# A transformer megakernel on one core: windowed attention's transposed scores as three float32r passes, with GpSimd making the low parts

## The chip, the cores and the metric

The kernel runs on one NeuronCore of a Trainium2 chip. The metric is the device time of one execution in microseconds; less is better. The time before is 2594.16 us, the median of three runs (2591.99 to 2595.44).

## The reference, cut to what matters

Six residual blocks run one after the other over 16 sequences of 256 tokens with 128 features. The change touches the first and the third, which are the same two-layer stack with windowed attention (8 heads of 64, window 64). Per layer:

```python
qkv = shift_token(x) @ wqkv
q, k = l2norm(q) * qs, l2norm(k) * ksc
q, k = rotary_xpos(q, k)                      # cosines, sines, a scale by position
sim = einsum('bhwid,bhwjd->bhwij', bq, bk)    # window of 64 queries, its 64 keys and the 64 before
sim = where(mask, -finfo.max, sim)
out = einsum('bhwij,bhwjd->bhwid', softmax(sim), bv)
x = x + out @ wo
h = layernorm(shift_token(x)) @ w1 + b1       # then a * gelu(g) @ w2 + b2, added to x
```

The other blocks (an attention with a distance bias, two mixtures of experts and a linear attention) are left as they are, but for one tile's place in memory.

## The kernel before, in words

Everything is laid out by hand: each engine has its own program, and semaphores order them. The feed-forward stage `ffn(f)` runs twice (f = 0 and 1). It walks over 32 items each time: layer 0 of the 16 sequences, then layer 1 of them. An item passes through three steps of the loop at once: in step k the engines project queries, keys and values of item k (`new`), do the attention of item k-1 (`mid`) and the feed-forward part of item k-2 (`old`). In layer 0, `pre` also normalises the input of a coming sequence. The order inside a step is written out in the loops at the end of each engine's `ffn`.

One step, as far as the change and the steps of the prediction touch it:

- TensorE turns (transposes) the rotated keys and queries of item i-1 (`qk_T`, L1284 and L1292) into PSUM, projects the first half of item i (`qk`, L1273 to L1275, float32r in three passes), projects the attention's output of item i-2 (`proj`, L1407), and computes plain scores (`scores`, L1329 masks, L1334 products in bf16), from which only the row maxima are taken.
- VectorE copies turned keys out of PSUM to `kT` (float32, L870) and from there to bf16, `kb` (L871), and raises `f_kb`. ScalarE copies turned queries to `qT` (L585) and to bf16, `qb` (L586), and raises `f_qsb`. Then ScalarE copies the projections of item i (`copy_qk`, L565).
- VectorE then does in this order: cosines of half 0 (L884), the residual (`resid`, L933), maxima of the plain scores (`s_max`, L908 and L913) with `y_center` (L939) between, the split of the maxima into two bf16 parts (`m_split`, L921 and L922), `y_normed` (L943), sums of squares (L890), `m_out` (L927), cosines of half 1 (L884), sums, `clip` (L895), `gated` (L950), two `qk_norm` (L901) and others.
- GpSimd multiplies by the sines (`sines`, L466, two instructions per half) and adds to the cosines (`rotated`, L474) for both halves of item i, and then splits the next item's input into a high and a low part (`split_h`, L491 and L493), ahead of which in layer 0 stands `normed` (L481).
- TensorE goes on with the feed-forward `up` (L1425), which waits for `y_normed`, and with the transposed scores (`scores_T`). For three groups of heads and columns it first adds offsets and masks in bf16 (`offsets`, L1355 and L1357), then the products `kT` by `qT` (`products`, L1363). These are float32 matmuls on 64 rows; two neighbouring heads lie on the two halves of the array. Offsets of group 2 wait for `gated`. Then come `down` (L1436) and the sums over the values (`attend`, L1388 and L1396), for which ScalarE makes exponentials (L593) of the transposed scores.

`link` is a helper that makes an engine wait for its own last instruction; `free(engine, semaphore, n)` is a wait that is left out for n <= 0. L1741 and L1739 belong to the linear attention, L818 to the preparation of weights.

Of the kernel before, what the change touches and what calls it, by code (L numbers as in the profile page):

```python
# [17 lines left out]
F32 = mybir.dt.float32  # L18
I32 = mybir.dt.int32
F32R = mybir.dt.float32r  # L20
BF16 = mybir.dt.bfloat16
# [7 lines left out]
P = 128  # L29
# [95 lines left out]
def build(nc, io, at):  # L125
    ctx = ExitStack()
    with ctx:
        def sb(name, shape, dt=F32, on=ctx):
            return on.enter_context(nc.sbuf_tensor(name, shape, dt))

        def sem(name):
            return ctx.enter_context(nc.semaphore(name))
# [64 lines left out]
        N_STAGE = at["slope_eye"][1]  # L197
        hh = [sb(f"h_hi{n}", [P, T], F32R) for n in range(2)]
        hl = [sb(f"h_lo{n}", [P, T], F32R) for n in range(2)]
        with ExitStack() as early:  # L200
            stage = sb("stage", [P, N_STAGE], on=early)
        scl = sqs[:, 0:8 * DH].rearrange("p (l g c d) -> p l g c d", l=DEPTH, g=2, c=2)
        with ExitStack() as ffn_small:
            kb, qb = sb("kT_bf", [P, 4, T], BF16, ffn_small), sb("qT_bf", [P, 4, T], BF16, ffn_small)
            V = [sb(f"v{n}", [P, TILES, INNER], F32, ffn_small) for n in range(2)]
            OT = sb("o_T", [P, 4, T], F32, ffn_small)
            G = sb("gelu", [P, HC, T], F32, ffn_small)
            U = sb("gated", [P, HC, T], F32, ffn_small)
        q_slots = [sb(f"q_slots{n}", [P, 4, T], F32R) for n in range(3)]
# [9 lines left out]
        with ExitStack() as ffn_only:  # L219
# [36 lines left out]
        wbuf = [work[0][:, EW * n:EW * (n + 1)] for n in range(5)]  # L256
        xtile = [sb(f"tile_x{n}", [P, HW]) for n in range(6)]
        xT = [sb(f"tile_xT{n}", [P, P]) for n in range(2)]
        gT = [sb(f"tile_g{n}", [P, EC, P]) for n in range(3)]
        yrow = [sb(f"tile_y{n}", [P, D]) for n in range(4)]  # L260
        o1, o2, o3 = 0, 4 * P, 4 * P + 2 * HC * P

# [17 lines left out]
        lbw, fold, chain = sem("lbw"), sem("fold"), sem("chain")  # L280
        f_y0, f_h, f_qk, f_cp, f_sq, f_cos, f_sin, f_sum, f_ss, f_ssm, f_rn, f_nrm = [sem(f"ffn_{n}") for n in
            ("y0", "h_split", "qk", "qk_sb", "sq", "cos", "sin", "rot", "ss", "ss_max", "rnorm", "qk_norm")]
        f_vsb, f_kT, f_qT, f_kb, f_qsb, f_s, f_smax, f_mlo, f_mT, f_mTs = [sem(f"ffn_{n}") for n in
            ("v_sb", "kT", "qT", "k_bf", "qT_sb", "s", "s_max", "m_lo", "mT", "mT_sb")]
        f_st, f_p, f_den, f_o, f_rec, f_on, f_proj, f_res = [sem(f"ffn_{n}") for n in
            ("st", "p", "den", "o", "rec", "o_norm", "proj", "resid")]
        f_mean, f_cen, f_lsq, f_var, f_rstd, f_norm, f_up, f_g, f_u, f_down, f_res2 = [sem(f"ffn_{n}") for n in
# [152 lines left out]
        def _(pool):  # L440
# [17 lines left out]
            def ffn(f):  # L458
                def sines(i, t):
                    l, _ = layer_of(i)  # L460
                    a = rA[:, t, :].rearrange("p (g h d) -> p g h d", g=2, h=HEADS)
                    b = rB[:, t, :].rearrange("p (g h d) -> p g h d", g=2, h=HEADS)
                    pool.wait_ge(f_cp, 2 * i + t + 1)
                    for h in range(2):
                        o_, i_ = slice(32 * h, 32 * h + 32), slice(32 - 32 * h, 64 - 32 * h)
                        last = pool.tensor_tensor(b[:, :, :, o_], a[:, :, :, i_],  # L466
                                                  tab[:, l, 1, t, :, o_].unsqueeze(2).to_broadcast([P, 2, HEADS, 32]),
                                                  ALU.mult)
                    last.then_inc(f_sin, 1)

                def rotated(i, t):
                    pool.wait_ge(f_sin, 2 * i + t + 1)
                    pool.wait_ge(f_cos, 2 * i + t + 1)
                    pool.tensor_tensor(rC[:, t, :], rC[:, t, :], rB[:, t, :], ALU.add).then_inc(f_sum, 1)  # L474

                def normed(s):
                    n = f * SEQS + s
                    free(pool, f_sum, 2 * (f * ITEMS + s))
                    pool.wait_ge(o_rstd, n + 1)
                    for h, (r, c) in enumerate(halves()):  # L480
                        pool.tensor_tensor(Y[r, s, c], ocen[r, :], osq[r, :], ALU.mult).then_inc(f_y0, 1)  # L481
                        pool.wait_ge(f_y0, 2 * n + h + 1)

                def split_h(i):
                    l, s = layer_of(i)
                    if l == 0:
                        pool.wait_ge(f_y0, 2 * (f * SEQS + s + 1))
                    else:
                        pool.wait_ge(f_res2, i - SEQS + 1)
                    free(pool, f_qk, 3 * (i - 1))  # L490
                    pool.tensor_copy(hh[i % 2][:, :], Y[:, s, 0:T]).then_inc(f_h, 1)  # L491
                    pool.wait_ge(f_h, 2 * i + 1)
                    pool.tensor_tensor(hl[i % 2][:, :], Y[:, s, 0:T], hh[i % 2][:, :].bitcast(F32), ALU.subtract)\  # L493
                        .then_inc(f_h, 1)

                for k in range(-1, ITEMS):
                    i = f * ITEMS + k
                    for t in range(TILES):
                        if k >= 0:
                            sines(i, t)  # L500
                            rotated(i, t)
                    if k + 1 < SEQS:
                        normed(k + 1)
                    if k + 1 < ITEMS:
                        split_h(i + 1)
# [44 lines left out]
        def _(act):  # L550
# [8 lines left out]
            def ffn(f):  # L559
# [21 lines left out]

                def copy_q(i):
                    act.wait_ge(f_qT, i + 1)
                    q = PS[:, 3:5, :]
                    act.activation(qT.rearrange("p (b c) t -> p b (c t)", b=2), q, ACT.Copy)  # L585
                    act.activation(qb[:, :, :].rearrange("p (b c) t -> p b (c t)", b=2), q, ACT.Copy).then_inc(f_qsb, 1)  # L586

                def exps(i, n):
                    act.wait_ge(f_st, 3 * i + n + 1)
# [217 lines left out]
        def _(dve):  # L807
# [59 lines left out]
            def ffn(f):  # L867
                def k_out(i):
                    dve.wait_ge(f_kT, i + 1)
                    link(dve.tensor_copy(kT.rearrange("p (b c) t -> p b (c t)", b=2), PS[:, 5:7, :]))  # L870
                    dve.tensor_copy(kb[:, :, :], kT).then_inc(f_kb, 1)  # L871

                def o_norm(i, a):
                    dve.wait_ge(f_o, 2 * i + a + 1)
# [379 lines left out]
        def _(pe):  # L1254
# [22 lines left out]
            def ffn(f):  # L1277
# [42 lines left out]
                def scores(i):  # L1320
# [10 lines left out]
                    for bs, hs, w, t, k0, _ in groups:  # L1331
                        for h in hs:
                            r, o = slice(64 * (h % 2), 64 * (h % 2) + 64), (h - hs[0]) // 2 * w
                            last = pe.matmul(PS[:, bs[h % 2], o:o + w], qb[r, h // 2, t * P:(t + 1) * P],  # L1334
                                             kb[r, h // 2, k0:k0 + w], start=False, stop=True, skip_group_check=True)
                        last.then_inc(f_s, 1)

                def m_T(i):
# [8 lines left out]
                def scores_T(i):  # L1347
# [10 lines left out]
                                      start=False, stop=False, skip_group_check=True)  # L1358

                    def products(bs, hs, w, j, i0, m):  # L1360
                        for h in hs:
                            r, o = slice(64 * (h % 2), 64 * (h % 2) + 64), (h - hs[0]) // 2 * w
                            last = pe.matmul(PS[:, bs[h % 2], o:o + w], kT[r, h // 2, j * P:(j + 1) * P],  # L1363
                                             qT[r, h // 2, i0:i0 + w], start=False, stop=True, skip_group_check=True)
                        last.then_inc(f_st, 1)

                    pe.wait_ge(f_mTs, i + 1)
                    pe.wait_ge(f_cp, min(2 * i + 4, 2 * ITEMS * (f + 1)))
                    offsets(*groups[0])
                    pe.wait_ge(f_vsb, min(i + 2, ITEMS * (f + 1)))  # L1370
# [449 lines left out]
```

## Time and profile before

| | |
|---|---|
| median of three runs | 2594.16 us |
| profiled execution, its own time | 2591.7 us |
| its span | 2589.9 us |
| TensorE busy | 2277.1 us, 88% |
| VectorE busy | 1718.9 us, 66% |
| ScalarE busy | 1463.9 us, 57% |
| GpSimd busy | 1089.9 us, 42% |

The span runs from the first to the last instruction of the profiled execution. The shares of busy time are averages over stages of different kinds; the two feed-forward stages lie at about 80 to 900 us and 1310 to 2125 us. In the views PE is TensorE, PEld its weight loads, DVE VectorE, ACT ScalarE, POOL GpSimd. A float32 matmul stands in the trace as two rows of instructions, a float32r or bf16 matmul as one.

### The profile page before, as it was taken

How to read it: one execution, taken by the hardware profiler on the slowest of the kernel's cores; microseconds unless marked ns; L12 is line 12 of the kernel's file. 1: busy time of each engine (PE TensorE's matmuls, PEld its weight loads, DVE VectorE, ACT ScalarE, POOL GpSimd, SP SyncE). 2: the span in 40 equal slices, each digit the busy share in tenths (PEclk: the TensorE clock that was granted, in tenths of full speed). 3: DMA queues.
4: the chain of work that ended last, by engine and by line, in shares of the span. 5: the costliest groups of instructions: out<-in, count | busy, mean ns of one | idle time of the engine just before them, and what ended most of it. 6: DMA issues, size and time to landing. Idle time of an engine off the chain costs nothing. (4 is left out here: it accounts for less than half of the span.)

```text
span 2589.9 us, 52641 instructions
## 1 busy us (share of the span) xinstructions
PE 2277.1 (88%) x21574; PEld 1715.4 (66%) x21574; DVE 1718.9 (66%) x2800; ACT 1463.9 (57%) x2382; POOL 1089.9 (42%) x800
## 2 busy tenths in 40 slices
PE   2799999999999779999789999999999984878576
PEld 1577777777777556666457777777777753766266
DVE  3677777777777457777367777777877844533544
ACT  0567676666666425556456767666666642434332
POOL 4655555565565100000065555556556504410432
PEclk8899999999999889999989999999999987999899
DMA  7000000089999000000000000000000012110013
GB/s 147 1 1 1 2 2 1 1 91 115 108 122 109 8 1 2 2 2 2 1 1 2 1 1 2 2 2 1 2 2 2 1 54 60 56 53 1 29 51 99
DMA packets 185425, 73.63 MB, mean 28 GB/s; under 512 B 79658, under 2 KB 181204, under 8 KB 185060
## 3 DMA queue, kind: packets, MB, share of 16 engines
q1 hardware_dynamic: 177172, 56.68, 18.3%
q0 software_dynamic: 5568, 10.12, 1.3%
q10 hardware_dynamic: 2448, 3.48, 0.6%
q8 instruction: 173, 2.83, 0.5%
q14 instruction: 64, 0.52, 0.1%
HBM read 24.05 MB, written 46.18 MB: 27 GB/s over the span
## 5 line engine op out<-in xcount | busy, mean ns | idle before, releaser
L466 POOL TENSOR_TENSOR work<-work,rot_tables 128x512 f32<-128x512 f32 x256 | 446.9, 1767 | 451.3 <-ACT work L565 451.3
L474 POOL TENSOR_TENSOR work<-work 128x1024 f32<-128x1024 f32 x128 | 305.2, 2385 | 13.0 <-DVE work L884 3.1
L884 DVE TENSOR_TENSOR work<-work,rot_tables 128x1024 f32<-128x1024 f32 x128 | 163.9, 1281 | 112.1 <-ACT work L565 112.1
L1039 DVE TENSOR_REDUCE small<-psum 128x4 f32<-128x1024 f32 x128 | 156.6, 1223 | 91.1 <-PE psum L1545 91.0
L1273 PE MATMUL psum<-qkv_w_hi,h_hi 128*128 128x512 f32 x384 | 182.8, 476 | 18.8 <-POOL h_lo L493 16.3
L1425 PE MATMUL psum<-centered,ffn_w 128*128 128x256 f32 x768 | 191.1, 400 | 6.5 <-DVE centered L943 2.9
L901 DVE TENSOR_TENSOR work<-work,small 128x1024 f32<-128x1024 f32 x128 | 159.6, 1249 | 51.2 <-ACT small L579 47.0
L676 ACT ACTIVATE work<-psum 128x1024 f32<-128x1024 f32 x128 | 131.1, 1024 | 100.5 <-PE psum L1552 100.5
L481 POOL TENSOR_TENSOR y_all<-centered,squared 64x256 f32<-64x256 f32 x64 | 48.3, 755 | 308.2 <-ACT squared L625 305.6
L1363 PE MATMUL psum<-work 64*128 64x128 f32 (+1 forms) x2048 | 175.8, 311 | 0.0
L1425 PEld LDWEIGHTS psum<-centered,ffn_w 128*128 128x128 f32 x768 | 146.2, 197 | 37.4 <-DVE centered L943 18.7
L1363 PEld LDWEIGHTS psum<-work 64*128 64x128 f32 x2048 | 144.7, 188 | 32.6 <-issue 32.6
L731 ACT ACTIVATE tile_g<-psum,work 128x128 f32<-128x128 f32 x312 | 89.0, 368 | 136.3 <-PE psum L1674 105.0
L1396 PE MATMUL psum<-work,v 128*32 128x192 f32 (+1 forms) x4096 | 162.6, 299 | 0.0
L593 ACT ACTIVATE work<-psum 128x768 f32<-128x768 f32 (+1 forms) x192 | 154.9, 872 | 5.4 <-PE psum L1363 5.1
L535 POOL DMA_INDIRECT h_area<-rows,position x64 | 62.5, 977 | 221.1 <-DVE position L1125 200.8
L890 DVE TENSOR_REDUCE small<-qk_squares 128x16 f32<-128x1024 f32 x128 | 154.7, 1209 | 0.4 <-ACT qk_squares L570 0.4
L1274 PE MATMUL psum<-qkv_w_lo,h_hi 128*128 128x512 f32 x384 | 153.4, 399 | 0.0
L1275 PE MATMUL psum<-qkv_w_hi,h_lo 128*128 128x512 f32 x384 | 153.1, 399 | 0.0
L585 ACT ACTIVATE work<-psum 128x1024 f32<-128x1024 f32 x64 | 65.7, 1026 | 144.6 <-PE psum L1292 144.6
L565 ACT ACTIVATE work<-psum 128x1024 f32<-128x1024 f32 x128 | 130.3, 1018 | 22.3 <-PE psum L1275 21.5
L570 ACT ACTIVATE qk_squares<-work 128x1024 f32<-128x1024 f32 x128 | 135.3, 1057 | 2.0
(280 smaller groups left out, 5695.2 us busy)
## 6 DMA issues: line engine op xcount, KB each, us to landing
h_area<-mean_weights SPq DMA_DIRECT2D x16, 2048.0 KB, 27.2
tile_x<-h_area SPq DMA_DIRECT2D x78, 64.5 KB
work<-y_tokens SPq DMA_DIRECT2D x8, 512.0 KB, 6.1
stage<-in_consts ACTq DMA_DIRECT2D x1, 3009.0 KB, 12.7
work<-in_x SPq DMA_DIRECT2D x4, 512.0 KB, 28.3
expert_w<-in_ew SPq DMA_DIRECT2D x1, 2048.0 KB
expert_w<-in_ew SPq DMA_DIRECT2D x8, 256.0 KB
out<-work SPq DMA_DIRECT2D x8, 256.0 KB, 3.5
```

The lines of the kernel that those rows point to most:

```text
L466: last = pool.tensor_tensor(b[:, :, :, o_], a[:, :, :, i_], tab[:, l, 1, t, :, o_].unsqueeze(2).to_broadcast([P, 2, HEADS, 32]), ALU.mult)
L474: pool.tensor_tensor(rC[:, t, :], rC[:, t, :], rB[:, t, :], ALU.add).then_inc(f_sum, 1)
L593: act.activation(PT[:, hs, a:a + w].rearrange("p (h b) j -> p b h j", b=2), PS[:, bs, 0:m * w].rearrange("p b (h j) -> p b h j", h=m), ACT ...
L884: dve.tensor_tensor(g(rC[:, t, :]), g(rA[:, t, :]), tab[:, l, 0, t, :, :].unsqueeze(2).to_broadcast([P, 2, HEADS, DH]), ALU.mult)\
L890: dve.tensor_reduce(sm[0][:, 16 * t:16 * t + 16], sq[:, t, :].rearrange("p (g d) -> p g d", d=DH), AX, ALU.add).then_inc(f_ss, 1)
L901: dve.tensor_tensor(c_, c_, sm[0][:, 96 + 16 * t:112 + 16 * t].unsqueeze(2).to_broadcast([P, 16, DH]), ALU.mult).then_inc(f_nrm, 1)
L1039: dve.tensor_reduce(dst, PS[:, 0:2, :].rearrange("p b (t j) -> p b t j", t=TILES), AX, ALU.max, negate=True).then_inc(a_smax, 1)
L1273: pe.matmul(out, hi, w_hi, start=True, stop=False)
L1274: pe.matmul(out, hi, w_lo, start=False, stop=False)
L1363: last = pe.matmul(PS[:, bs[h % 2], o:o + w], kT[r, h // 2, j * P:(j + 1) * P], qT[r, h // 2, i0:i0 + w], start=False, stop=True, skip_gro ...
L1396: last = pe.matmul(PS[32 * q:32 * q + 32, (4, 2)[a], z * T + lo:z * T + hi], V[i % 2][:, j, d:d + 32], PT[:, 4 * a + q, src:src + hi - lo] ...
L1425: last = pe.matmul(PS[:, b, o:o + T], fw[:, l, o2 + c * P:o2 + (c + 1) * P], ycen[:, :], start=True, stop=True)
```

## The change

The bf16 copies of the turned keys and queries are replaced by float32r tiles `kh` and `qh`, written by the same VectorE and ScalarE instructions. GpSimd gets a new step `lows`, which subtracts them from `kT` and `qT` and writes the float32r tiles `kl` and `ql`; it raises a new semaphore `f_low`. The plain scores use `kh` and `qh`. The products of the transposed scores are three float32r passes: high by high, low keys by high queries, high keys by low queries. TensorE waits for `f_low` ahead of the transposed scores, and VectorE and ScalarE wait for it before they overwrite `kT` and `qT`. The tiles `V` and `o_T` move out of the part of memory that later stages reuse, and `gT` of the mixture of experts is put into `V`'s memory.

```diff
-            kb, qb = sb("kT_bf", [P, 4, T], BF16, ffn_small), sb("qT_bf", [P, 4, T], BF16, ffn_small)
+            kh, kl = [sb(f"kT_{n}", [P, 4, T], F32R, ffn_small) for n in ("hi", "lo")]
+            qh, ql = [sb(f"qT_{n}", [P, 4, T], F32R, ffn_small) for n in ("hi", "lo")]
...
-        gT = [sb(f"tile_g{n}", [P, EC, P]) for n in range(3)]
+        gT = [V[n // 2][:, n % 2, :].rearrange("p (c t) -> p c t", c=EC) for n in range(3)]
...
+                def lows(i):
+                    pool.wait_ge(f_kb, i + 1)
+                    free(pool, f_st, 3 * i)
+                    pool.tensor_tensor(kl[:, :, :], kT, kh[:, :, :].bitcast(F32), ALU.subtract).then_inc(f_low, 1)
+                    pool.wait_ge(f_qsb, i + 1)
+                    pool.tensor_tensor(ql[:, :, :], qT, qh[:, :, :].bitcast(F32), ALU.subtract).then_inc(f_low, 1)
+
-                for k in range(-1, ITEMS):
+                for k in range(-1, ITEMS + 1):
                     i = f * ITEMS + k
+                    if 0 <= k - 1:
+                        lows(i - 1)
+                    if k == ITEMS:
+                        break
                     for t in range(TILES):
                         if k >= 0:
                             sines(i, t)
...
                 def copy_q(i):
                     act.wait_ge(f_qT, i + 1)
+                    free(act, f_low, 2 * i)
...
-                    act.activation(qb[:, :, :].rearrange("p (b c) t -> p b (c t)", b=2), q, ACT.Copy).then_inc(f_qsb, 1)
+                    act.activation(qh[:, :, :].rearrange("p (b c) t -> p b (c t)", b=2), q, ACT.Copy).then_inc(f_qsb, 1)
...
                     dve.wait_ge(f_kT, i + 1)
+                    free(dve, f_low, 2 * i)
                     link(dve.tensor_copy(kT.rearrange("p (b c) t -> p b (c t)", b=2), PS[:, 5:7, :]))
-                    dve.tensor_copy(kb[:, :, :], kT).then_inc(f_kb, 1)
+                    dve.tensor_copy(kh[:, :, :], kT).then_inc(f_kb, 1)
...
-                            last = pe.matmul(PS[:, bs[h % 2], o:o + w], qb[r, h // 2, t * P:(t + 1) * P],
-                                             kb[r, h // 2, k0:k0 + w], start=False, stop=True, skip_group_check=True)
+                            last = pe.matmul(PS[:, bs[h % 2], o:o + w], qh[r, h // 2, t * P:(t + 1) * P],
+                                             kh[r, h // 2, k0:k0 + w], start=False, stop=True, skip_group_check=True)
...
-                        for h in hs:
-                            r, o = slice(64 * (h % 2), 64 * (h % 2) + 64), (h - hs[0]) // 2 * w
-                            last = pe.matmul(PS[:, bs[h % 2], o:o + w], kT[r, h // 2, j * P:(j + 1) * P],
-                                             qT[r, h // 2, i0:i0 + w], start=False, stop=True, skip_group_check=True)
+                        for h in range(hs[0], hs[-1] + 1, 2):
+                            for n, (k_, q_) in enumerate(((kh, qh), (kl, qh), (kh, ql))):
+                                for e in range(2):
+                                    r, o = slice(64 * e, 64 * e + 64), (h - hs[0]) // 2 * w
+                                    last = pe.matmul(PS[:, bs[e], o:o + w], k_[r, h // 2, j * P:(j + 1) * P],
+                                                     q_[r, h // 2, i0:i0 + w], start=False, stop=n == 2,
+                                                     skip_group_check=True)
                         last.then_inc(f_st, 1)
 
                     pe.wait_ge(f_mTs, i + 1)
+                    pe.wait_ge(f_low, 2 * i + 2)
```

On GpSimd, one step of the first stage, before. L481 is `normed`, L491 and L493 `split_h`, L466 and L474 `sines` and `rotated`:

```order
L481 TENSOR_TENSOR y_all<-centered,squared 64x256 x2
L491 CAST h_hi<-y_all 128x256
L493 TENSOR_TENSOR h_lo<-y_all,h_hi 128x256
L466 TENSOR_TENSOR work<-work,rot_tables 128x16x32 x2
L474 TENSOR_TENSOR work<-work 128x1024
L466 TENSOR_TENSOR work<-work,rot_tables 128x16x32 x2
L474 TENSOR_TENSOR work<-work 128x1024
```

The same step of the changed kernel (L500 and L502 are `lows`; `sines` is L467 there, `rotated` L475):

```order
L482 TENSOR_TENSOR y_all<-centered,squared 64x256 x2
L492 CAST h_hi<-y_all 128x256
L494 TENSOR_TENSOR h_lo<-y_all,h_hi 128x256
L500 TENSOR_TENSOR kT_lo<-work,kT_hi 128x1024
L502 TENSOR_TENSOR qT_lo<-work,qT_hi 128x1024
L467 TENSOR_TENSOR work<-work,rot_tables 128x16x32 x2
L475 TENSOR_TENSOR work<-work 128x1024
```

Two instructions of 128x1024 are new, and all sines and sums of the item stand behind them.

On TensorE, groups 0 and 1 of the transposed scores, before (the last mask of the offsets, then the products; `work` holds `kT` and `qT`):

```order
L1357 MATMUL psum<-masks_bf,eye_bf 128x512
L1363 MATMUL psum<-work 128x192 x4
L1363 MATMUL psum<-work 128x128 x8
L1355 MATMUL psum<-mT,m_rows_bf 128x192 x2
```

And in the changed kernel, the first head pair of group 0 and the first of group 1:

```order
L1371 MATMUL psum<-masks_bf,eye_bf 128x512
L1379 MATMUL psum<-qT_hi,kT_hi 128x192 x2
L1379 MATMUL psum<-qT_hi,kT_lo 128x192 x2
L1379 MATMUL psum<-qT_lo,kT_hi 128x192 x2
...
L1379 MATMUL psum<-qT_hi,kT_hi 128x128 x2
L1379 MATMUL psum<-qT_hi,kT_lo 128x128 x2
L1379 MATMUL psum<-qT_lo,kT_hi 128x128 x2
```

Each pair of matmuls on neighbouring heads has become three pairs; nothing else moves on TensorE.

## Rows read from the trace of the kernel before

**Rows 1.** Windows: busy us (x instructions) of PE, PEld, DVE, ACT, POOL; PE clock, DMA
```profile
100.00:480.00 380.00, 374.99 (x3619) 280.35 (x3618) 280.15 (x415) 257.39 (x398) 213.19 (x148) 1.00 0.01 1
2130.00:2300.00 170.00, 111.44 (x826) 95.34 (x824) 80.80 (x245) 65.73 (x189) 71.89 (x71) 0.87 0.26 72
```
**Rows 2.** Timeline of PE, starts of `down`; start us, us, engine line op
```profile
703.21 1.56 PE L1436 MATMUL psum<-gated,ffn_w 128*128 128x256 f32 x6
727.53 1.56 PE L1436 MATMUL psum<-gated,ffn_w 128*128 128x256 f32 x6
...
231.72 1.56 PE L1436 MATMUL psum<-gated,ffn_w 128*128 128x256 f32 x6
```
**Rows 3.** Timeline, a step of layer 1, from the key cast on
```profile
711.11 0.69 DVE L871 CAST kT_bf<-work 128x1024 bf16<-128x1024 f32 x1
...
713.17 1.22 DVE L884 TENSOR_TENSOR work<-work,rot_tables 128x1024 f32<-128x1024 f32 x1 [1.37 <-ACT work L565]
713.22 3.54 POOL L466 TENSOR_TENSOR work<-work,rot_tables 128x512 f32<-128x512 f32 x2 [9.51 <-ACT work L565]
...
714.31 0.85 DVE L933 TENSOR_TENSOR y_all<-y_all,psum 64x256 f32<-64x256 f32 x2
...
716.84 2.38 POOL L474 TENSOR_TENSOR work<-work 128x1024 f32<-128x1024 f32 x1
716.85 1.81 DVE L913 TENSOR_REDUCE small<-psum 128x4 f32<-128x768 f32 x2
...
718.70 0.56 DVE L921 CAST m_neg<-small 128x16 bf16<-128x16 f32 x1
...
719.29 0.17 DVE L922 TENSOR_TENSOR m_neg<-small,m_neg 128x16 bf16<-128x16 f32 x1
719.38 0.42 DVE L943 TENSOR_TENSOR centered<-centered,squared 128x256 f32<-128x256 f32 x1
...
719.86 2.42 PE L1425 MATMUL psum<-centered,ffn_w 128*128 128x256 f32 x10
...
721.18 1.27 DVE L884 TENSOR_TENSOR work<-work,rot_tables 128x1024 f32<-128x1024 f32 x1
```
**Rows 4.** One line's instructions, L884: duration ns min/median/max, first and last start
```profile
L884 DVE TENSOR_TENSOR work<-work,rot_tables x128: 1203/1226/3097, 69.4 to 2071.0; 128x1024 f32<-128x1024 f32 x128
```
**Rows 5.** Timelines of POOL and of DVE in the first items
```profile
76.29 2.47 POOL L466 TENSOR_TENSOR work<-work,rot_tables 128x512 f32<-128x512 f32 x2
78.84 3.21 POOL L474 TENSOR_TENSOR work<-work 128x1024 f32<-128x1024 f32 x1
...
77.65 2.20 DVE L901 TENSOR_TENSOR work<-work,small 128x1024 f32<-128x1024 f32 x1 [0.95 <-ACT small L579]
```
**Rows 6.** Groups by form: busy us, mean ns of one, idle before (DVE, then PEld)
```profile
L818 DVE CAST attn_w_hi<-work 128x1024 fp32r<-128x1024 f32 x1 | 0.7, 694 | 0.0
...
L1274 PEld LDWEIGHTS psum<-qkv_w_lo,h_hi 128*128 128x128 f32 x384 | 74.0, 193 | 7.7
...
L1334 PEld LDWEIGHTS psum<-kT_bf,qT_bf 64*128 64x128 bf16 x1024 | 32.1, 94 | 20.3 <-issue 20.3
...
L1741 PEld LDWEIGHTS psum<-one_col,work 128*128 128x128 f32 x64 | 8.4, 192 | 0.0
```
**Rows 7.** Timeline of the step before, its transposed scores
```profile
699.86 1.81 PE L1363 MATMUL psum<-work 64*128 64x192 f32 x24
...
700.17 1.27 DVE L950 SCALAR_TENSOR_TENSOR gated<-psum,b,gelu 128x256 f32<-128x256 f32 x3 [0.70 <-ACT gelu L614]
...
701.60 0.34 PE L1355 MATMUL psum<-mT,m_rows_bf 128*128 128x192 bf16 x2
...
702.36 0.92 PE L1363 MATMUL psum<-work 64*128 64x192 f32 x8
```
**Rows 8.** Timeline, a step of layer 0
```profile
214.77 0.69 DVE L871 CAST kT_bf<-work 128x1024 bf16<-128x1024 f32 x1
...
223.15 0.42 DVE L943 TENSOR_TENSOR centered<-centered,squared 128x256 f32<-128x256 f32 x1
```

More of the change, by code:

```diff
@@ L199, in build @@
         hl = [sb(f"h_lo{n}", [P, T], F32R) for n in range(2)]
+        V = [sb(f"v{n}", [P, TILES, INNER], F32) for n in range(2)]
+        OT = sb("o_T", [P, 4, T], F32)
         with ExitStack() as early:
@@ L203, in build @@
         with ExitStack() as ffn_small:
-            kb, qb = sb("kT_bf", [P, 4, T], BF16, ffn_small), sb("qT_bf", [P, 4, T], BF16, ffn_small)
-            V = [sb(f"v{n}", [P, TILES, INNER], F32, ffn_small) for n in range(2)]
-            OT = sb("o_T", [P, 4, T], F32, ffn_small)
+            kh, kl = [sb(f"kT_{n}", [P, 4, T], F32R, ffn_small) for n in ("hi", "lo")]
+            qh, ql = [sb(f"qT_{n}", [P, 4, T], F32R, ffn_small) for n in ("hi", "lo")]
             G = sb("gelu", [P, HC, T], F32, ffn_small)
@@ L282, in build @@
             ("y0", "h_split", "qk", "qk_sb", "sq", "cos", "sin", "rot", "ss", "ss_max", "rnorm", "qk_norm")]
-        f_vsb, f_kT, f_qT, f_kb, f_qsb, f_s, f_smax, f_mlo, f_mT, f_mTs = [sem(f"ffn_{n}") for n in
-            ("v_sb", "kT", "qT", "k_bf", "qT_sb", "s", "s_max", "m_lo", "mT", "mT_sb")]
+        f_vsb, f_kT, f_qT, f_low, f_kb, f_qsb, f_s, f_smax, f_mlo, f_mT, f_mTs = [sem(f"ffn_{n}") for n in
+            ("v_sb", "kT", "qT", "low", "k_hi", "qT_sb", "s", "s_max", "m_lo", "mT", "mT_sb")]
         f_st, f_p, f_den, f_o, f_rec, f_on, f_proj, f_res = [sem(f"ffn_{n}") for n in
```

## The prediction

> **What bounds the kernel now.** I read the windows first: in a stretch of the feed-forward stage TensorE is busy 375 of 380 us at full clock, and VectorE, ScalarE and GpSimd have room [rows 1]. That stage is 64 items (two passes of 32: 16 sequences by two layers). The starts of the down projection give an item of layer 1 24.32 us (703.21 to 727.53) [rows 2]. So the first thought is that only TensorE's matmuls count. The timeline of one item corrects it [rows 3]. From ScalarE's copy of item i's first half (it ends the wait of VectorE's L884 at 713.17) VectorE works without a gap: cosines, residual, the maxima, the split of the maxima (L921, L922) and y_normed (L943), which ends at 719.80, and TensorE's `up` starts 0.06 behind it, at 719.86. There VectorE sets the pace. From `up` to the next L871 TensorE does, by way of `down`.
>
> The rows that decide are those of GpSimd beside VectorE. L884 takes 1203 to 1226 ns mostly, but up to 3097 [rows 4]. In the first items one sees what makes it long: L901, another product of two operands in SBUF, starts at 77.65 inside a pair of GpSimd products that ends at 76.29 + 2.47 = 78.76, and ends at 79.85, 1.09 behind them; the GpSimd sum that starts at 78.84 then takes 3.21 instead of 2.38, and ends 2.20 behind L901 [rows 3, 5]. So each waits for the other's running instruction, and who asked first goes first. L921, a small cast, does it too: it takes 0.56 and ends at 719.26, just behind GpSimd's L474 (716.84 + 2.38 = 719.22). VectorE's maxima and sums that read PSUM alone (L913, under the same L474) are not held. I call this the port. Today GpSimd is idle at 713.17 when L884 starts, and idle from 719.22 when L922 and L943 run.
>
> **The change part by part.** *GpSimd's lows.* Per item two sums of 128x1024 with both operands in SBUF are added, the shape of L474 at 2.38 us [rows 3]. They stand ahead of the sines of item i, and the first waits only for VectorE's high part of the keys. I take the high part at the cast's old time: a cast of 128x1024 to float32r took 694 ns and L871 0.69 [rows 3, 6]. In layer 1, step by step:
> - L871 ends at 711.80; kl, 0.05 later, runs 711.85 to 714.23. VectorE's L884 asks at 713.17 and gets the port at 714.23, so it ends 1.08 later, at 715.31 (before 714.39). ScalarE's copies could grow by a microsecond before that showed.
> - ql gets the port at 715.31 and ends 2.20 later, at 717.51; the two sines L466 take 2.47 as a pair when nothing holds them [rows 5]: to 719.98.
> - VectorE: from the start of L933 to that of L921 it was 714.31 to 718.70, 4.39 us. Now L933 starts at 715.23 and L921 asks at 719.62, under the sines. It ends at 720.01, and L922, 0.21 behind it as before, at 720.22.
> - GpSimd's next sum (L474) starts 0.08 behind the sines, at 720.06; L943 follows at 720.13 and stands behind it. The sum gets the port at 720.22 and holds it 2.20, to 722.42. L943 then needs 0.28 for its 256 columns: **722.70 in place of 719.80**. If the sum should win against L922 as well, L922 and L943 both run behind it and the end is the same.
> - `up` starts at 722.76. GpSimd's second sines follow L943: 1.13 and 1.23, to 725.06. L884 of the second half asks about 1.38 behind L943's end (721.18 against 719.80), at 724.08, and waits for 725.06: end 726.14. The sum L474 behind it: 726.21 to 728.59. The small L895 asks while it runs, ends at 728.62, and gated (L950, 1.27) at 729.87. The gelu is earlier: L950 ran 4.63 behind `up` before, which gives 727.39.
> - TensorE would be ready for group 2's offsets 6.06 behind `up` as before (719.86 to 725.92, which is the start at 701.60 [rows 7] plus 24.32), plus 0.42 (next part): 729.24. It waits for gated to 729.92. Offsets and products of group 2 took 703.21 - 701.60 = 1.61: **`down` at 731.53 in place of 727.53, 4.00 us per item**.
>
> In layer 0, L871 starts at 214.77, so kl at 215.51 (0.69 and 0.05 on); L943 ends 10.85 behind kl's start, as above, at 226.36, where it was 223.57 [rows 8]; `down` 8.83 later, 235.19, in place of 231.72 [rows 2]: 3.47 us.
>
> *TensorE's products.* 12 matmuls, 24 rows, in 1.81 us for groups 0 and 1 [rows 7] become 36 rows, in 18 pairs (the two heads of a pair use the two halves of the array side by side). Each must load its weights. Where the moving operand is one column (L1741) 64 loads in runs of four are busy 8.4 us: 0.525 for four, the last 0.192 of it, so 0.11 apart [rows 6]. 18 pairs by 0.112 and about 0.2 to drain make 2.2, an estimate: +0.42. Group 2 stays at 0.92 [rows 7] within 0.05: six pairs by 0.112, 0.2 to drain and 0.1 for a first load in front of which nothing runs. If the loads had the pace of the bf16 scores, three single passes over the 2560 columns of an item would cost about 2.0 us (the 16 loads of one pass, L1334, are busy 32.1 us / 64 = 0.50 [rows 6]; 0.5 to drain twice), against 1.81 + 0.92 now: -0.7. I take the slow load: a float32r load (L1274) takes 193 ns in the trace, like the float32 of L1741 at 192, and bf16 94 [rows 6]. The Trainium skill (TensorE: Matmul & The Clock Gate, section Weight-path perf modes — Fast Weight Load (FWL) and DoubleRow) gives the fast load to 128 weights whose type is not FP32; read literally it would include float32r, and the product term would be -0.7 us. The 193 ns row speaks against it. The +0.42 is hidden by the wait for gated (729.24 against 729.87); without that cover it costs 27 us over 64 items.
>
> *The plain scores* load float32r too: eight pairs by 0.112 in place of 0.50 in all [rows 6], about +0.4. Their first group is needed by L908 only after L933, which is now 0.9 later: nothing. Uncovered, its four pairs cost some 0.25 more in the 32 items of layer 0, 8 us (in layer 1 L933 ended late enough to hide it). *f_low waits* of TensorE, ScalarE and VectorE: ql ends at 717.51, and the transposed scores begin past 724: nothing. *gT in V's memory* moves no instruction: nothing.
>
> **The sum.** 32 x 4.00 + 32 x 3.47 = 239 us. The profiled execution took 2591.7 us, so 2830.7; the median of the runs shown is 2.5 higher, so **2833**.
>
> **The rivals.**
> 1. *L943 slips through.* VectorE's L943 follows L922 with no wait between, and might keep the port. Then it ends at 720.50; the sum at 722.70, L884 at 723.78, sines 724.91 and 726.14, L895 behind them at 726.17, gated 727.42; TensorE is ready at 727.04. `down` at 729.08: +1.55 per item, 99 us: 2693. For it: 0.07 separates the two starts. Against: a GpSimd instruction that had asked was let in first between other pairs. 0.15.
> 2. *GpSimd holds nobody in the new place.* Then only TensorE's terms count: 27 + 8, 2629. The 3097 ns row speaks against it. 0.07.
> 3. *Faster.* It takes both: GpSimd doesn't hold VectorE, and the float32r loads run at the bf16 pace, 0.06 per pair or less. Then the products save 0.7 less 0.1 for the plain scores: 64 x 0.6 = 38 us, 2556. It decides at a pair pace of about 0.09, where products cost what they do now. 0.03.
> 4. *Worse.* TensorE now idles over 2 us ahead of `up` and is busy about 85% of an item. In a stretch where it is busy 66% the granted clock is 0.87 [rows 1]. Should it fall to 0.95, some 1.1 us per item come on top: 2900. Or L943 loses to one more sine. 0.08.
>
> The forecast itself has 0.60; mixtures between rivals 1 and the forecast (one collision missed) 0.07.
>
> **How the numbers follow.** The time is the forecast's, 2833. The range 2685 to 2890 takes in the forecast, the mixtures, rival 1 and most of rival 4, and leaves out rivals 2 and 3. A difference of 0.2%, 5 us, is what runs of this kernel can tell. Faster 0.04 (rival 3 and a little for what I don't see), same 0.02, slower 0.94.
>
> **What would show it.** Right: the first lows start 0.05 behind the key cast; L884 of the first half takes about 2.1 us; L943 takes 2.5; TensorE idles over 2 us ahead of `up`; items at 28.3 and 29 us; pairs of the products 0.11 apart. Wrong: L943 at 0.42, items of 25 to 26 us (rivals 1 and 2), or product pairs under 0.09 apart (rival 3).

## The result, and the profile after

| | before | after |
|---|---|---|
| median, us | 2593.07 (4 runs) | 2848.28 (2842.05 to 2850.21, 4 runs) |
| ratio, 95% interval | | 1.0985 (1.0958 to 1.1012) |
| span of the profiled execution, us | 2589.9 | 2847.9 |
| mean granted clock | 0.957 | 0.938 |

The change costs 255 us; forecast were 239. Lines move: the cosines are L898 now, the split of the maxima L935 and L936, `y_normed` L957, `clip` L909, `gated` L964, `m_out` L941, `up` L1443, `down` L1454, the offsets L1369 and L1371; `sines` L467, `rotated` L475, `lows` L500 and L502.

The groups of the changed kernel (busy us, mean ns of one, then idle time of the engine ahead of them):

```profile
L957 DVE TENSOR_TENSOR centered<-centered,squared 128x256 f32<-128x256 f32 x64 | 156.5, 2445 | 4.5 <-ACT squared L621 4.4
L898 DVE TENSOR_TENSOR work<-work,rot_tables 128x1024 f32<-128x1024 f32 x128 | 214.0, 1672 | 112.9 <-ACT work L577 112.9
L885 DVE CAST kT_hi<-work 128x1024 fp32r<-128x1024 f32 x64 | 44.4, 694 | 2.2
L1443 PE MATMUL psum<-centered,ffn_w 128*128 128x256 f32 x768 | 235.8, 470 | 133.7 <-DVE centered L957 133.7
```

`y_normed`, a product of 256 columns, now takes 2.45 us at the mean (0.42 in [rows 3]), and TensorE sits idle ahead of `up` for 133.7 us, 2.1 us an item, waiting for it. The high part costs 694 ns, as assumed.

The timeline of one item of layer 1, which answers to [rows 2, 3, 7]:

```profile
751.34 1.56 PE L1454 MATMUL psum<-gated,ffn_w 128*128 128x256 f32 x6
...
759.24 0.69 DVE L885 CAST kT_hi<-work 128x1024 fp32r<-128x1024 f32 x1
...
760.01 2.36 POOL L500 TENSOR_TENSOR kT_lo<-work,kT_hi 128x1024 fp32r<-128x1024 f32 x1 [8.48 <-DVE kT_hi L885]
...
762.33 3.35 POOL L502 TENSOR_TENSOR qT_lo<-work,qT_hi 128x1024 fp32r<-128x1024 f32 x1
...
765.64 2.53 POOL L467 TENSOR_TENSOR work<-work,rot_tables 128x512 f32<-128x512 f32 x2
...
767.75 0.44 DVE L935 CAST m_neg<-small 128x16 bf16<-128x16 f32 x1
768.23 0.17 DVE L936 TENSOR_TENSOR m_neg<-small,m_neg 128x16 bf16<-128x16 f32 x1
768.24 2.37 POOL L475 TENSOR_TENSOR work<-work 128x1024 f32<-128x1024 f32 x1
768.32 2.58 DVE L957 TENSOR_TENSOR centered<-centered,squared 128x256 f32<-128x256 f32 x1
...
770.58 4.04 POOL L467 TENSOR_TENSOR work<-work,rot_tables 128x512 f32<-128x512 f32 x2
...
770.95 2.86 PE L1443 MATMUL psum<-centered,ffn_w 128*128 128x256 f32 x12 [2.17 <-DVE centered L957]
...
772.28 1.20 DVE L898 TENSOR_TENSOR work<-work,rot_tables 128x1024 f32<-128x1024 f32 x1
...
774.65 0.18 DVE L909 TENSOR_SCALAR small<-small 128x32 f32<-128x32 f32 x1
774.70 2.38 POOL L475 TENSOR_TENSOR work<-work 128x1024 f32<-128x1024 f32 x1
774.74 1.26 DVE L964 SCALAR_TENSOR_TENSOR gated<-psum,b,gelu 128x256 f32<-128x256 f32 x3
...
777.43 0.34 PE L1369 MATMUL psum<-mT,m_rows_bf 128*128 128x192 bf16 x2
...
779.04 1.56 PE L1454 MATMUL psum<-gated,ffn_w 128*128 128x256 f32 x6
```

GpSimd never rests from the first `lows` on, so its sum L475 starts at 768.24, just when VectorE comes to `y_normed` at 768.32. The sum won by 0.08 us, and `y_normed` ended 0.29 behind it (768.24 + 2.37 = 770.61; 768.32 + 2.58 = 770.90). `down` to `down` is 27.70 us, 24.32 before [rows 2].

Not every item is like this one. Windows over the twelve matmuls of `up`, here and in the next item (columns as in [rows 1]):

```profile
770.90:773.80 2.90, 2.85 (x14) 2.44 (x15) 2.90 (x4) 2.12 (x5) 2.90 (x2) 1.00 0.65 1
798.70:802.40 3.70, 3.70 (x11) 3.06 (x12) 3.67 (x5) 2.17 (x4) 3.62 (x3) 0.64 1.14 158
```

```profile
798.66 4.47 PE L1443 MATMUL psum<-centered,ffn_w 128*128 128x256 f32 x12 [2.16 <-DVE centered L957]
...
808.43 1.56 PE L1454 MATMUL psum<-gated,ffn_w 128*128 128x256 f32 x6
```

In the second the granted clock of the window was 0.64, a mean of time at 1.2 GHz and at 2.4, and `up` took 4.47 us in place of 2.86: that item has 29.39 us (779.04 to 808.43). In layer 0 such items are the rule: `down` starts at

```profile
197.72 1.56 PE L1454 MATMUL psum<-gated,ffn_w 128*128 128x256 f32 x6
226.45 1.56 PE L1454 MATMUL psum<-gated,ffn_w 128*128 128x256 f32 x6
256.85 1.56 PE L1454 MATMUL psum<-gated,ffn_w 128*128 128x256 f32 x6
```

28.73 us, then 30.40. By the starts of `down`, 22 items of layer 0 and 6 of layer 1, counted over both passes, have the longer form, 1.69 us each: 47 us. (The last two items of a pass have an `up` of over 4 us in the kernel before as well, and are not counted.)

### The profile page after: what moved, and what is told of

It reads as the page before. It is cut to its first block and busy times, and to the rows that moved or that the text cites. A ratio compares the mean times of both kernels' runs of the same rounds, so it can differ in the third digit from the quotient of the medians.

```text
span 2847.9 us, 55006 instructions
## 1 busy us (share of the span) xinstructions
PE 2393.3 (84%) x22598; PEld 1821.0 (64%) x22598; DVE 1912.9 (67%) x2800; ACT 1484.0 (52%) x2382; POOL 1418.4 (50%) x928
## 5 line engine op out<-in xcount | busy, mean ns | idle before, releaser
L467 POOL TENSOR_TENSOR work<-work,rot_tables 128x512 f32<-128x512 f32 x256 | 419.1, 1657 | 8.2 <-ACT work L577 8.2
L1443 PE MATMUL psum<-centered,ffn_w 128*128 128x256 f32 x768 | 235.8, 470 | 133.7 <-DVE centered L957 133.7
L500 POOL TENSOR_TENSOR kT_lo<-work,kT_hi 128x1024 fp32r<-128x1024 f32 x64 | 151.5, 2368 | 348.0 <-DVE kT_hi L885 348.0
L475 POOL TENSOR_TENSOR work<-work 128x1024 f32<-128x1024 f32 x128 | 305.2, 2385 | 13.0 <-DVE work L898 3.1
L898 DVE TENSOR_TENSOR work<-work,rot_tables 128x1024 f32<-128x1024 f32 x128 | 214.0, 1672 | 112.9 <-ACT work L577 112.9
L1443 PEld LDWEIGHTS psum<-centered,ffn_w 128*128 128x128 f32 x768 | 174.0, 233 | 176.4 <-DVE centered L957 146.0
L502 POOL TENSOR_TENSOR qT_lo<-work,qT_hi 128x1024 fp32r<-128x1024 f32 x64 | 210.8, 3294 | 0.0
L972 DVE SCALAR_TENSOR_TENSOR y_all<-psum,b,y_all 64x256 f32<-64x256 f32 x128 | 62.0, 484 | 196.6 <-PE psum L1454 195.7
L689 ACT ACTIVATE work<-psum 128x1024 f32<-128x1024 f32 x128 | 131.2, 1025 | 102.3 <-PE psum L1570 102.3
L957 DVE TENSOR_TENSOR centered<-centered,squared 128x256 f32<-128x256 f32 x64 | 156.5, 2445 | 4.5 <-ACT squared L621 4.4
L744 ACT ACTIVATE v<-psum,work 128x128 f32<-128x128 f32 x312 | 89.2, 369 | 134.2 <-PE psum L1692 134.2
```

The costliest lines, as they stand in the source:

```text
L467: last = pool.tensor_tensor(b[:, :, :, o_], a[:, :, :, i_], tab[:, l, 1, t, :, o_].unsqueeze(2).to_broadcast([P, 2, HEADS, 32]), ALU.mult)
L502: pool.tensor_tensor(ql[:, :, :], qT, qh[:, :, :].bitcast(F32), ALU.subtract).then_inc(f_low, 1)
L898: dve.tensor_tensor(g(rC[:, t, :]), g(rA[:, t, :]), tab[:, l, 0, t, :, :].unsqueeze(2).to_broadcast([P, 2, HEADS, DH]), ALU.mult)\
L957: dve.tensor_tensor(ycen[:, :], ycen[:, :], ysq[:, :], ALU.mult).then_inc(f_norm, 1)
L1443: last = pe.matmul(PS[:, b, o:o + T], fw[:, l, o2 + c * P:o2 + (c + 1) * P], ycen[:, :], start=True, stop=True)
```

## The experiments

The theory was the forecast's: VectorE's instructions with SBUF operands and GpSimd's wait for each other, and after the change that wait falls on `y_normed`; beside it, the products' weight loads. The rivals were TensorE's own work, GpSimd's longer work as such, and the lows' own traffic.

**Products alone: e1_fp32_products.** The changed kernel with the products of before, lows kept.

```diff
-  for n, (k_, q_) in enumerate(((kh, qh), (kl, qh), (kh, ql))): ...
+  for h in hs: ... pe.matmul(PS[...], kT[r, h // 2, ...], qT[r, h // 2, i0:i0 + w], ...)
```

> The changed kernel with the transposed scores' products put back to one float32 matmul per head; the high and low parts are still made, the low ones by GpSimd as in the change, and read by nobody. Theory (GpSimd's hold of the port makes the item longer, and in the profile after, TensorE no longer waits for gated ahead of group 2): the time stays far above before and loses only the products' own 0.4 us per item, 2848 - 27 = about 2821. If the products are hidden, as the prediction had it: 2848. Rival (the three passes are what costs): back near 2600.

Measured: 2791.12 us (2788.82 to 2799.67), 1.0787 of before (1.0760 to 1.0814), 57 less than the changed kernel. That is more than either case had. Items of layer 1 have 27.31 us in place of 27.71, so the products cost 0.40 us an item, 26 in all, and nothing hides it: the offsets of group 2 follow the products at once, long after `gated` (in the item above `gated` ends at 776.00, the offsets start at 777.43). Of the other 31 us, 24 are 14 fewer items with the long `up` (14 of the 28 are left, none in layer 1), and most of the rest lies between the two passes. That the term is hidden was wrong, its size (0.42) right.

**No lows: e2_no_lows.** `lows` and the waits on `f_low` are taken out; all three passes use `kh` and `qh`.

```diff
-                    if 0 <= k - 1:
-                        lows(i - 1)
-  ((kh, qh), (kl, qh), (kh, ql))
+  ((kh, qh), (kh, qh), (kh, qh))
```

> The changed kernel without GpSimd's lows; the three passes all read the high parts, so the low parts are left out of the scores. Theory (the port): GpSimd's pattern is that of before, L957 takes 0.42 again, and only TensorE's terms stay: 27 us for the products and up to 8 for the plain scores, 2620 to 2630. Rival (the passes cost): near 2848.

Measured: 2622.92 us (2619.61 to 2626.22), 1.0129 (1.0106 to 1.0153). Items 24.74 and 26.0 us, +0.42 and +0.55. So 225 of the 255 us come with the lows, and about 30 with TensorE's part. Three single passes are slower than the float32 products here even where the low parts cost nothing.

**Shorter holds: e3_pieces.** Lows and sums in four instructions of 256 columns.

```diff
-  pool.tensor_tensor(rC[:, t, :], rC[:, t, :], rB[:, t, :], ALU.add).then_inc(f_sum, 1)
+  for z in range(4):
+      w_ = slice(z * 256, (z + 1) * 256)
+      last = pool.tensor_tensor(rC[:, t, w_], rC[:, t, w_], rB[:, t, w_], ALU.add)
+  last.then_inc(f_sum, 1)
```

> The changed kernel with GpSimd's lows and sums of the rotation cut in four instructions of 256 columns each: the same bytes, by 16 shorter instructions per item. If a GpSimd instruction holds VectorE until it ends, the longest hold falls from 2.4 to about 0.6 us, L957 takes 0.5 to 1.1 in place of 2.58, L898 of the first half 1.3 to 1.8 in place of 2.16, and an item is 1 to 1.6 us longer than before: 2655 to 2700. If the two engines share bandwidth, or it is GpSimd's total work, the time stays at 2848 or rises.

Measured: 2710.73 us (2695.74 to 2711.36), 1.0449 (1.0418 to 1.0480), just above the range. The gain came in another way than I meant (timelines of VectorE, L943 the second half of the split and L964 `y_normed`, and of GpSimd):

```profile
764.83 1.19 DVE L943 TENSOR_TENSOR m_neg<-small,m_neg 128x16 bf16<-128x16 f32 x1
765.94 0.41 DVE L964 TENSOR_TENSOR centered<-centered,squared 128x256 f32<-128x256 f32 x1
```

```profile
764.68 1.30 POOL L467 TENSOR_TENSOR work<-work,rot_tables 128x512 f32<-128x512 f32 x1
766.07 4.15 POOL L477 TENSOR_TENSOR work<-work 128x256 f32<-128x256 f32 x4
```

Here the second sine holds the 16-column L943 until it ends, and `y_normed`, with no gap behind L943, is 0.13 ahead of the first piece. It isn't held a quarter as long, it isn't held at all: 0.41 us. That made order, not length, the thing to test.

**Pieces in the kernel before: e4_before_pieces.** The same cut of the sums in the kernel before.

> The kernel before with GpSimd's sums of the rotation (L474) cut in four instructions of 256 columns. In before, L921 waits 0.37 us for L474's end in most items, on the chain that VectorE paces. If the hold ends with the instruction, L921 takes 0.2 to 0.5 and 0.1 to 0.3 us per item are won: 2575 to 2590. If not, 2593 or a little above, for the fixed cost of more instructions.

Measured: 2603.49 us (2595.19 to 2607.73), 1.0048 (1.0029 to 1.0067): a miss. Groups:

```profile
L925 DVE TENSOR_TENSOR m_neg<-small,m_neg 128x16 bf16<-128x16 f32 x64 | 41.3, 646 | 2.2
...
L924 DVE CAST m_neg<-small 128x16 bf16<-128x16 f32 x64 | 16.6, 260 | 2.2
```

The cast is shorter (0.56 in [rows 3]), but the next piece catches the instruction behind it. Many short holds caught more than one long one.

**What the lows do: e9_memsets.** GpSimd's lows become memsets of about their length (four and five an item, of 256 to 1024 columns), the low parts left out of the products.

```diff
-  pool.tensor_tensor(kl[:, :, :], kT, kh[:, :, :].bitcast(F32), ALU.subtract).then_inc(f_low, 1)
+  pool.memset(kl[:, 0:2, :].bitcast(F32), 0.0).then_inc(f_low, 1)
+  ...
```

> The two lows are replaced by memsets into the same tiles, which read nothing and keep GpSimd from the sines for as long as the lows did (2.4 and 3.1 us an item); the products use high parts in all three passes, so the low parts are left out of the scores. Theory (what costs is that the sum L475 now runs when VectorE's y_normed is due; the lows only push it there): y_normed still takes about 2.5 us, items stay within 0.4 us of 27.7 in layer 1, and the time is 2848 within 25. The first cosines (L898) fall back to 1.2 us, since a memset needs no operand. Rival (the lows' own two-operand reads are what VectorE pays for): y_normed 0.42 again, items near 24.7 us as without the lows, 2625 to 2650.

Measured: 2781.48 us (2775.86 to 2784.34), 1.0738 (1.0721 to 1.0755): outside both. The two layers went different ways. Layer 0 (L948 second half of the split, L969 `y_normed`), VectorE and GpSimd:

```profile
244.25 0.17 DVE L948 TENSOR_TENSOR m_neg<-small,m_neg 128x16 bf16<-128x16 f32 x1
244.35 2.57 DVE L969 TENSOR_TENSOR centered<-centered,squared 128x256 f32<-128x256 f32 x1
```

```profile
241.67 2.52 POOL L467 TENSOR_TENSOR work<-work,rot_tables 128x512 f32<-128x512 f32 x2
244.26 2.37 POOL L475 TENSOR_TENSOR work<-work 128x1024 f32<-128x1024 f32 x1
```

Layer 1:

```profile
781.18 1.20 DVE L948 TENSOR_TENSOR m_neg<-small,m_neg 128x16 bf16<-128x16 f32 x1
782.30 0.41 DVE L969 TENSOR_TENSOR centered<-centered,squared 128x256 f32<-128x256 f32 x1
```

```profile
779.83 2.52 POOL L467 TENSOR_TENSOR work<-work,rot_tables 128x512 f32<-128x512 f32 x2
782.42 2.51 POOL L475 TENSOR_TENSOR work<-work 128x1024 f32<-128x1024 f32 x1
```

Layer 0 is the theory to the letter: nothing reads for the lows any more, and `y_normed` still takes 2.57, items 30.6 us. So the lows' own reads are not what costs there; they only push the sum onto `y_normed`. In layer 1 the split began 0.96 us behind the sines' start (780.79, the cast, against 779.83) and in layer 0 1.40 (243.07 against 241.67); there L948 was the one they held (1.20), `y_normed` came 0.12 ahead of the sum, and the item has 25.95 us. This is the forecast's rival 1. Against the kernel before, layer 0 is 5.1 us an item longer, the clock's 1.69 included, and layer 1 only 1.6. The first cosines (L910) take 1.22 to 1.23 us beside the memsets: those hold nobody.

**VectorE first: e8_yield.**

```diff
                 def rotated(i, t):
                     pool.wait_ge(f_sin, 2 * i + t + 1)
                     pool.wait_ge(f_cos, 2 * i + t + 1)
+                    if t == 0:
+                        free(pool, f_norm, i - 1)
```

> One wait is added to the changed kernel: GpSimd's sum of half 0 (L475) starts only when y_normed of the item in flight is done. Theory (collision of the sum with y_normed): y_normed falls from 2.58 to about 0.45 us and TensorE's up starts some 2.1 us earlier; sines and sum of half 1 are late by about 0.4 us and collide with cosines of half 1, which gated may pass on. Items of 25.5 to 26.0 us in layer 1 and 26.4 to 27.0 in layer 0, and fewer clock drops: 2660 to 2710. Rival (GpSimd's own longer work, and not the collision, sets the pace): a wait more can only delay it, 2848 or more.

Measured: 2696.52 us (2682.49 to 2703.35), 1.0416 (1.0382 to 1.0450): as the theory said. `y_normed` takes 0.42, items 26.26 and 26.86 us (the first 0.26 above what was expected), and no item has the long `up` but the last two of a pass, as in the kernel before. An added wait on an engine off the path saves 152 us, so GpSimd's amount of work is not the bound.

**The clock: e6_filler.** Eight dummy matmuls in TensorE's idle time; the wait for the maxima moves ahead of them.

```diff
+                    pe.wait_ge(f_smax, ...)
+                    for _ in range(8):
+                        pe.matmul(PS[:, 4, :], eyeb[:, :], masks[:, 0:512], start=True, stop=True)
                     pe.wait_ge(f_norm, i + 1)
-                    pe.wait_ge(f_smax, ...)
```

> The changed kernel with eight dummy bf16 matmuls of 512 columns ahead of TensorE's wait for y_normed, into a bank that up overwrites; they fill the 2.2 us in which TensorE idles there. Theory (the idle time ahead of up is what lets the granted clock fall in some items, each 1.67 us longer): no item of the feed-forward stages with up at half clock, layer 0 at 28.75 and layer 1 at 27.7, 2848 less 50 = 2798 (2785 to 2812). Rival (the clock falls for another reason, or the fillers delay up): within 10 us of 2848, or above.

Measured: 2791.87 us (2789.02 to 2797.42), 1.0792 (1.0775 to 1.0810): as the theory said. TensorE still idles 0.35 us ahead of `up` in place of 2.17, layer 0 has 28.75 us in every item but the last four, which are shorter in the kernel before too, layer 1 27.71 with one exception (28.20); windows of this kernel:

```profile
120.00:500.00 380.00, 370.51 (x3489) 270.44 (x3486) 285.21 (x373) 232.70 (x357) 259.27 (x160) 1.00 0.01 1
```

In the changed kernel the same window has clock 0.96. Dummy work bought 56 us: the 47 of the long items, and 7 between the passes.

**The split in a reduction: e7_reduce_cast, in the kernel before.** The small cast is held by the sum [rows 3]; a reduction over an axis of one writes the same values.

```diff
-                    link(dve.tensor_copy(mneg[:, :, 0:HEADS], mx))
+                    link(dve.tensor_reduce(mneg[:, :, 0:HEADS], mx.unsqueeze(3), AX, ALU.max))
```

> The kernel before, with the cast of the maxima to bf16 (L921, 0.56 us, held until GpSimd's sum ends) made by a tensor_reduce over an axis of one. Theory (casts and sums of SBUF operands wait for GpSimd's running instruction, reductions do not): the cast takes about 0.2 us, L922 behind it is held instead for a rest of 0.1 to 0.2; some 0.2 us an item: 2578 (2572 to 2586). Rival (every VectorE instruction that reads SBUF is held, the reduction too): 2590 within 4.

Measured: 2577.38 us (2575.38 to 2583.97, 6 runs), 0.9961 (0.9947 to 0.9974), the fastest version here, and close to the 2578 expected. In the items it is half of what was expected: 24.22 us in layer 1 and 25.35 in layer 0, where the kernel before has 24.32 and 25.48, and the two passes are shorter by 3.0 and 2.5 us. The rest of the 12 us lies outside the passes, where the edit changes nothing, and no run explains it. The reduction takes 170 ns (the cast had 538), and the instruction behind it is held for the rest:

```profile
L922 DVE TENSOR_TENSOR m_neg<-small,m_neg 128x16 bf16<-128x16 f32 x64 | 22.0, 344 | 2.2
L921 DVE TENSOR_REDUCE m_neg<-small 128x16 bf16<-128x16 f32 x64 | 10.9, 170 | 2.2
```

The Trainium skill (SBUF — State Buffer, section Who interferes with whom) says that copies, casts and scalar operations can take the ports that the two engines share, that a sum or product with both inputs in SBUF contends with GpSimd's reads, and that a reduction never contends on this chip; for the cast and the reduction this run agrees, 538 ns against 170 in the same place. By the same section of the Trainium skill a GpSimd operation that reads nothing does not hold such a product, which the 1.23 us beside the memsets (e9) bear out.

**The same line in the changed kernel: e10_after_reduce.** It moves VectorE's requests by a quarter of a microsecond, and nothing else.

> The changed kernel with one edit: the cast of the maxima (L935, 0.44 us, held by the second sine) is a tensor_reduce over an axis of one, which waited for nothing in the kernel before. Theory (who asks first goes first, and 0.1 us decides): the small difference L936 is now the one that the second sine holds; y_normed follows it without a gap and has asked before GpSimd's sum L475, so it takes 0.42 us and the sum waits; up starts about 2.3 us earlier in every item. Items of 25.6 to 26.2 us in layer 1 and 26.3 to 27.0 in layer 0: 2650 to 2710. Rival (the sum wins all the same, or waiting goes by the length of GpSimd's work and not by order): y_normed still 2.5 us and at most 0.1 us an item less, 2840 to 2850.

Measured: 2669.76 us (2665.13 to 2670.34), 1.0314 (1.0286 to 1.0341), 179 us less than the changed kernel by one small instruction. Timelines of VectorE, GpSimd and TensorE:

```profile
774.83 0.17 DVE L935 TENSOR_REDUCE m_neg<-small 128x16 bf16<-128x16 f32 x1
775.03 0.25 DVE L936 TENSOR_TENSOR m_neg<-small,m_neg 128x16 bf16<-128x16 f32 x1
775.26 0.42 DVE L957 TENSOR_TENSOR centered<-centered,squared 128x256 f32<-128x256 f32 x1
```

```profile
772.72 2.53 POOL L467 TENSOR_TENSOR work<-work,rot_tables 128x512 f32<-128x512 f32 x2
775.32 2.59 POOL L475 TENSOR_TENSOR work<-work 128x1024 f32<-128x1024 f32 x1
```

```profile
775.79 2.86 PE L1443 MATMUL psum<-centered,ffn_w 128*128 128x256 f32 x12
```

`y_normed` starts 0.06 ahead of the sum, and now the sum is the one that takes longer. Items have 25.82 and 26.49 us, and the mean of `y_normed` over the 64 items is 425 ns.

This is the working of the forecast's rival 1, step by step: the sum that waited ends later and holds the second cosines (L898, 1.94 us in place of 1.20), the second sines hold `clip`, and TensorE waits for `gated`:

```profile
780.16 1.24 DVE L909 TENSOR_SCALAR small<-small 128x32 f32<-128x32 f32 x1
782.63 0.34 PE L1369 MATMUL psum<-mT,m_rows_bf 128*128 128x192 bf16 x2 [0.29 <-DVE gated L964]
```

An item of layer 1 has 1.50 us more than before, where rival 1 had 1.55: 0.74 ahead of `up`, where the first cosines are held by kl (2.15 us in place of 1.22), and 0.77 behind it (`up` to `down` is 8.44 us, 7.67 before), mostly the products' 0.42 and this 0.29.

**Both: e11_both.** This line and e8's wait.

> As e10, and GpSimd's sum of half 0 also waits for y_normed as in e8. Theory: the order that e8 forces is the one that e10 reaches by itself, so the two differ by 10 us at most, and both lie near e8's 2697. Rival (e8's wait cost something of its own, or e10's order is reached in some items alone): e11 more than 15 us from e10.

Measured: 2684.91 us (2681.11 to 2690.76), 1.0370 (1.0336 to 1.0403). It is 15 us above e10, just on the rival's side: e8's wait does cost something, 26.12 us an item of layer 1 against 25.82. It holds the sum until 0.17 behind the end of `y_normed`, where in e10 the sum already stands in line, and the second cosines, which wait for the sum, take 2.24 us in place of 1.94; behind them TensorE waits 0.60 us for `gated`, where it waited 0.29. What pays is the order, not the wait that forces it.

## Why the prediction was right

The mechanism and the place were right and the time within 16 us; below the sum, two terms were off.

| step, layer 1 | forecast | measured |
|---|---|---|
| kl behind the key cast | 0.05 | 0.08 |
| end of the first cosines behind kl's end | 1.08 | 1.08 |
| end of `y_normed` behind kl's start | 10.85 | 10.89 |
| `up` to the offsets of group 2, TensorE ready | 6.48 | 6.48 |
| end of `gated` behind the start of `up` | 7.11 | 5.05 |
| `up` to `down` | 8.77 | 8.09 |
| item | +4.00 | +3.38 |

(The second line is from the item of 787.71, where L500 ends at 790.08 and L898 at 791.16; the others from the item shown.)

- **The first half**, from kl to `y_normed`, came out as worked: +2.90 forecast, +2.96 measured (751.34 to 770.95 is 19.61, and 703.21 to 719.86 [rows 2, 3] is 16.65).
- **The second half failed.** The step was "L884 of the second half asks about 1.38 behind L943's end (721.18 against 719.80), at 724.08, and waits for 725.06", with the small `clip` held behind it. Neither was held: L898 asked 1.38 behind, as forecast, but took 1.20 and passed GpSimd's second sine, which waited (the pair took 4.04), and `clip` came 0.05 ahead of the sum. `gated` was so early that it covered nothing, and **"the +0.42 is hidden by the wait for gated"** fell with it; e1 prices it at 0.40. So the item gains 0.42 there in place of 1.10. The second sine by itself, changed kernel:

```profile
771.99 2.63 POOL L467 TENSOR_TENSOR work<-work,rot_tables 128x512 f32<-128x512 f32 x1
```

  It is recorded 0.29 ahead of L898 (772.28), and yet it is the one that takes longer (2.63 us, where 1.28 is usual), so here the forecast's rule "who asked first goes first" fails by the recorded starts. The kernel before doesn't show it. There the pair of sines takes long too, but its second sine is recorded 0.14 behind L884 (721.18 [rows 3]), as the rule has it:

```profile
720.09 3.49 POOL L466 TENSOR_TENSOR work<-work,rot_tables 128x512 f32<-128x512 f32 x2 [0.86 <-ACT work L565]
...
721.32 2.26 POOL L466 TENSOR_TENSOR work<-work,rot_tables 128x512 f32<-128x512 f32 x1
```

  In layer 0 the same error is smaller, +3.3 us where 3.47 was forecast.
- **The clock** was rival 4, given 0.08, worked out at 2900 (ten above the range's upper end) and left out of the sum. It came in 28 items, 47 us, and e6 shows the cause by its cure: with TensorE's idle time filled the long `up` is gone. The gap of over 2 us ahead of `up` was forecast; its price was weighed too low. Why only 28 items have the long `up`, with the same gap in nearly all of them, isn't shown.
- **The sum.** Between the first and the last `down` the passes grow by 121.7 and 121.1 us; the long items are 47 of that, the lengths of the items 196. The forecast had 239 for them: 0.6 too much in an item of layer 1, 0.2 in layer 0, and the last two steps of a pass, with fewer items in flight, grow by only 1.0 to 1.5 us together. The clock's 47 and some 15 us outside the passes (7 ahead of the first `down`, where the first steps of a pass already run, 12 between the passes, 4 less behind them; not traced further) make up for it. So that 255 is so near to 239 is in part luck: errors of either sign nearly cancel.
- **The products and the plain scores**: pairs 0.11 apart, as forecast from the 192 ns loads, and the float32r loads of the products take 188 to 189 ns. Rival 3 is out, and so is the rule of the Trainium skill (TensorE: Matmul & The Clock Gate, section Weight-path perf modes — Fast Weight Load (FWL) and DoubleRow) read literally, by which float32r would load fast: bf16 loads take 94 ns [rows 6]. The plain scores cost nothing in layer 1 and up to 0.13 us in layer 0, by e2's 0.55 against 0.42.
- **Rival 1** had 0.15, for a race decided by 0.07 us. The race is real: e3, e9 in layer 1 and e10 fall on its side, the changed kernel and e9 in layer 0 on the forecast's. Its worked item, 1.55 us more, is e10's in layer 1 (1.50); it took the same for layer 0, which has 1.01, and so its time was 2693 and e10 has 2670. In the changed kernel the sum won by 0.08 us: that the forecast's branch came, and not this one, was partly luck too.

What stays open: why the second cosines pass the second sine. It isn't an exception of one item: 60 of the changed kernel's second cosines start 0.29 to 0.31 us behind a sine and take 1.20, and in e3 L905 (767.74) passes a piece of the sum recorded at 767.59. Yet `y_normed`, 0.08 behind the sum, is held. So the recorded starts alone don't tell who gets in first; no run was made for it.

## What to carry to other kernels

Before work is added to GpSimd, list VectorE's instructions whose operands are all in SBUF and that stand on the critical path, and ask which GpSimd instruction will run when each comes due: a product of 0.42 us took 2.5 here. Such a collision is settled by order and not by length, though the recorded starts don't always show the order; a wait that lets the critical one go first, or a reduction in place of a small cast ahead of it, gave back 150 to 180 us of 255, and cutting GpSimd's work in pieces made the kernel before slower. Where TensorE comes to idle for 2 us in every item, price its clock too.

## What the runs showed of the hardware that was not expected

- A tenth of a microsecond between two requests is worth 2.2 us an item by the hold, and the clock comes on top (e9: 5.1 us an item in layer 0, 1.6 in layer 1).
- VectorE's instruction that follows another without a gap was let in before GpSimd's next one, whose start stands 0.06 to 0.13 us later (e3, e9, e10); where the sum's start stood 0.08 us earlier, it was not (the changed kernel).
- `m_out`, a cast that reads PSUM, took 0.40 us under a running sum of GpSimd (e10), where the SBUF cast L921 is held until the sum ends (0.56 us [rows 3]).
- Matmuls whose results nobody uses, in a gap of 2.2 us, kept the granted clock at 1.00 where it had been 0.96, and made a kernel 56 us faster (e6).
- A reduction in the place of a small SBUF cast isn't held: 170 ns against 538 (e7).
